# Scattering expert results to token rows, and max tiles of 512 and 205 keys under a new head order

## What is computed

```python
xn = layernorm(x)
# attention, 16 heads of 16: all 2048 queries, but only 717 keys are allowed
cam = (pos < 205) | (pos >= 2048 - 512)
attn = softmax(where(cam, (rope(q) @ rope(k).T) / 4, -inf))
a = (attn @ v) @ Wo.T + bo
# experts: 8 of them, inner width 176, each token goes to its best one
expert, weight = top-1 index of (xn @ router.T), first of softmax(top 2)
f = weight * ((silu(gate[expert](xn)) * up[expert](xn)) @ down[expert].T)
out = x + a + f
```

## Time and profile before

| | busy us | share of the span |
|---|---|---|
| TensorE matmul (PE) | 370.9 | 94% |
| VectorE (DVE) | 322.2 | 82% |
| ScalarE (ACT) | 270.2 | 68% |
| GpSimd (POOL) | 65.6 | 17% |
| chain that ended last: on PE | | 83% |
| TensorE clock granted | 0.996 on average | |

### The profile page before, as it was taken

One profiled execution on the slowest core, in us unless ns is written; L12 is line 12 of the kernel. 1 busy time (PEld: TensorE's weight loads), 2 busy tenths in 40 slices (PEclk: granted clock), 3 DMA queues, 4 the chain that ended last, 5 costly groups with the idle time before them and its releaser, 6 DMA issues.

```text
span 394.7 us, 12245 instructions
## 1 busy us (share of the span) xinstructions
PE 370.9 (94%) x4646; PEld 194.1 (49%) x4646; DVE 322.2 (82%) x549; ACT 270.2 (68%) x537; POOL 65.6 (17%) x82
## 2 busy tenths in 40 slices
PE   0999999999999999999999999999999999997896
PEld 0765566766655443444444444445454444432265
DVE  5769789997759888988888888888888898874566
ACT  2534666564448878778787787878888888886910
POOL 5003734431000213032130321300000000000000
PEclk9999999999999999999999999999999999998999
DMA  7998556755111213032130321302102022095626
GB/s 238 407 384 215 145 169 200 215 171 157 41 58 54 70 32 95 11 94 63 41 88 14 99 55 46 92 11 71 55 21 70 25 52 56 17 204 105 101 54 213
DMA packets 30920, 42.53 MB, mean 108 GB/s; under 512 B 10724, under 2 KB 25700, under 8 KB 30048
## 3 DMA queue, kind: packets, MB, share of 16 engines
q1 hardware_dynamic: 29000, 36.71, 32.5%
q0 software_dynamic: 1872, 5.11, 5.1%
HBM read 27.75 MB, written 13.67 MB: 105 GB/s over the span
## 4 chain that ended last, share of the span: by engine, by line
PE 83%; DMA 5%; DVE 4%; issue 3%; ACT 2%; SPq 2%; DVEq 0%; ACTq 0%
PE ps L735 19%; PE ps L713 18%; PE ps L653 17%; PE ps L601 7%; PE ps L528 5%; PE ps L614 5%; PE ps L772 4%; DVE mx L1025 3%; DMA softmax_sums<-o_st 2%; DMA bqk<-bqk_in 2%; PE ps L639 2%; PE ps L517 1%; PE ps L587 1%; PE ps L626 1%; PE ps L510 1%
## 5 line engine op out<-in xcount | busy, mean ns | idle before, releaser
L1025 DVE TENSOR_REDUCE mx<-ps 128x1 f32<-128x717 f32 x232 | 198.6, 899 | 30.6 <-PE ps L653 30.1
L735 PE MATMUL ps<-q_op,k_op 98*32 98x512 bf16 (+1 forms) x1472 | 129.7, 383 | 3.6 <-DMA q_op<-neg_row 1.6
L1307 ACT ACTIVATE probs<-ps 128x512 f32<-128x512 f32 x192 | 103.1, 598 | 19.9 <-PE ps L735 18.1
L653 PE MATMUL ps<-k_op,q_op 96*32 96x512 bf16 (+1 forms) x1856 | 111.2, 315 | 0.4 <-DVE mx L1025 0.3
L653 PEld LDWEIGHTS ps<-k_op,q_op 96*32 96x32 bf16 x1856 | 50.7, 96 | 56.3 <-issue 25.3
L735 PEld LDWEIGHTS ps<-q_op,k_op 98*32 98x32 bf16 (+1 forms) x1472 | 42.3, 96 | 67.0 <-ACT probs L1307 15.0
L713 PE MATMUL ps<-probs,v_op 128*32 128x512 f32 x384 | 50.6, 595 | 0.2 <-ACT o_st L1298 0.2
L1307 ACT ACTIVATE dn<-ps 77x512 f32<-77x512 f32 x64 | 34.8, 595 | 11.6 <-PE ps L735 11.6
L457 POOL COPY v_op<-v_all 128x192 f32<-128x192 f32 x16 | 7.0, 446 | 202.7 <-PE ps L713 202.7
L1307 ACT ACTIVATE gu<-ps 128x512 f32<-128x512 f32 x64 | 34.5, 599 | 9.1 <-PE ps L735 9.1
L1307 ACT ACTIVATE wqk<-ps 128x512 f32<-128x512 f32 x64 | 33.5, 599 | 8.1 <-PE ps L735 8.1
(11 more groups left out here) (127 smaller groups left out, 366.0 us busy)
## 6 DMA issues: line engine op xcount, KB each, us to landing
q_parts<-parts SPq DMA_DIRECT2D x12, 256.0 KB
sorted_results<-ys SPq DMA_DIRECT2D x23, 128.0 KB
q_op<-q_parts SPq DMA_DIRECT2D x15, 192.0 KB
gu<-gu_in SPq DMA_DIRECT2D x1, 2816.0 KB, 13.7
tab<-tab_in SPq DMA_DIRECT2D x1, 2048.0 KB, 11.6
sorted_rows<-xn SPq DMA_DIRECT2D x4, 512.0 KB, 6.1
out<-x_sb SPq DMA_DIRECT2D x8, 256.0 KB, 2.4
q_op<-q_parts SPq DMA_DIRECT2D x15, 128.0 KB
```

The lines of the kernel that those rows point to most:

```text
L653: ins = pe.matmul(ps[r:r + CW, at + c0:at + c0 + n], q_op[slot][0:KR, P * t + r:P * t + r + CW], k_op[slot][0:KR, c0:c0 + n], start=True, ...
L735: ins = pe.matmul(bank(4 + u % RING)[r:r + w, :], k_op[k][:, c0 + r:c0 + r + w], q_op[k][:, QB * b:QB * b + QB], start=True, stop=True)
L1025: dve.tensor_reduce(mx[:, slot, t:t + 1], ps[:, at:at + NK], AX.X, ALU.max).then_inc(max_reduced, 1)
L1307: act.activation(prob[c][0:rows, QB * b:QB * b + QB], bank(4 + u % RING)[0:rows, :], ACT.Exp, scale=SCALE).then_inc(exp_done, 1)
```

## The change

- Expert results. POOL scatters the rows of slot t with an indirect DMA from `ys` to the token's own row of `y_dram`; rows that hold no token go to row 0, and tokens have rows 1 to 2048. `result_row` holds these indices; `token_of` is the same less one, floored at zero. The scatters lag eight slots behind the gathers on POOL, each waits for its `ys` and for the landing of the scatter before. In the heads SP loads `y_dram` plainly to `y_tok` in four DMAs of 512 KB, two after `head_step(0)` and two after `head_step(1)`; on POOL only the bias add is left.
- Max tiles. The 512-column part of a tile is a step of its own (M, banks 0 and 1 by turns), the 205-column parts of two neighbouring tiles are one step (N, bank 2), and the turn of the negated maxima is a step (T), with bank 3 to itself. VectorE takes 16 maxima over 512 and 8 over 2 x 205 per head, and joins the two sets in one 16-element instruction (`join`).
- The head order, and one of its own for head 14, in which only eight M and four N remain. ScalarE copies the last head's output after unit 3 instead of unit 4.
- SP: the `load_attn` of heads 0-7 goes behind `head_step(14)`.

The core of the diff:

```diff
-ORDER = ("MSMSSSMP" + "MSMSSSMP" + "SMMSSP" + "SMSMSSSMP" + "MSMSSSMP" + "SMMSSSP")
+ORDER = ("SMSMSNSMP" + "MNSSMSMP" + "NSSMSMNSP" + "SMMSSNSP" + "TMSSMNSSMSMP" + "SNSMSMSNP")
+ORDER_14 = ("SMSMSNSMP" + "MNSSMSMP" + "NSSMSMNSP" + "SSTSSP" + "SSSSP" + "SSSSSP")
+LAG = 8
...
-            def store_ys(t):
-                sp.wait_ge(ys_ready, t + 1)
-                sp.dma_start(y_dram[t * P:t * P + P, :], ys[t % XR][:]).then_inc(ys_stored[t % XR], 16)
+            def load_results(g):
+                rows = y_dram[1 + 4 * P * g:1 + 4 * P * (g + 1), :].rearrange("(t p) d -> p t d", p=P)
+                sp.dma_start(y_tok[:, 4 * g:4 * g + 4, :], rows).then_inc(results_in, 16)
...
             for s in range(2, NSLOT):
-                store_ys(s - 2)
...
             load_neg(0, 0)
-            for t in range(NSLOT - 2, NSLOT):
-                store_ys(t)
             head_step(0, 0, first=True)
+            for n in range(XR):
+                sp.wait_ge(ys_stored[n], 16 * len(range(n, NSLOT, XR)))
+            for g in range(2):
+                load_results(g)
             head_step(1, 1)
+            for g in range(2, 4):
+                load_results(g)
...
+            head_step(14, 2, load=False)
             load_attn(0, HEADS // 2, attn_in[0])
-            head_step(14, 2, load=False)
             load_attn(HEADS // 2, HEADS - 2, attn_in[1])
...
+            def scatter(t):
+                pool.wait_ge(ys_ready, t + 1)
+                if t > 0:
+                    pool.wait_ge(ys_stored[(t - 1) % XR], ((t - 1) // XR + 1) * 16)
+                pool.indirect_dma_start(
+                    out=y_dram, out_offset=bass.IndirectOffsetOnAxis(ap=result_row[:, t:t + 1], axis=0),
+                    in_=ys[t % XR][:], in_offset=None
+                ).then_inc(ys_stored[t % XR], 16)
...
+            for t in range(LAG, NSLOT + LAG):
+                if t < NSLOT:
+                    gather(t)
+                scatter(t - LAG)
...
-            def gather_result(t):
-                pool.indirect_dma_start(
-                    out=y_tok[:, t, :], out_offset=None, in_=y_dram,
-                    in_offset=bass.IndirectOffsetOnAxis(ap=row_of[:, t:t + 1], axis=0)
-                ).then_inc(gathered, 16)
+            def add_bias(t):
                 pool.tensor_tensor(x_sb[:, t, :], x_sb[:, t, :], bvo[:, HID:2 * HID], ALU.add
...
-            def max_tile(h, t, slot):
-                pe.wait_ge(max_reduced, h * NT + t - 1)
-                at = 1024 * (t % 2)
-                if t == 3:
-                    pe.wait_ge(neg_copied, h)
-                if t == 1:
-                    turn_neg(h - 1, (slot - 1) % RING)
-                for c0, n in ((0, 512), (512, NK - 512)):
+            def max_wide(h, t, slot):
+                if wide_count(h, t) >= 2:
+                    pe.wait_ge(wide_reduced, wide_count(h, t) - 1)
+                for r in range(0, P, CW):
+                    ins = pe.matmul(bank(t % 2)[r:r + CW, :], q_op[slot][0:KR, P * t + r:P * t + r + CW],
+                                    k_op[slot][0:KR, 0:NWIDE], start=True, stop=True)
+                ins.then_inc(wide_scored, 1)
+            def max_tail(h, pair, slot):
+                if tail_count(h, pair) >= 1:
+                    pe.wait_ge(tail_reduced, tail_count(h, pair))
+                for n in range(2):
+                    t = 2 * pair + n
                     for r in range(0, P, CW):
...
+                                        k_op[slot][0:KR, NWIDE:NK], start=True, stop=True)
+                ins.then_inc(tail_scored, 1)
...
-            def reduce_tile(h, t, slot):
-                dve.wait_ge(max_scored, h * NT + t + 1)
-                at = 1024 * (t % 2)
-                dve.tensor_reduce(mx[:, slot, t:t + 1], ps[:, at:at + NK], AX.X, ALU.max
+            def reduce_pair(h, pair, slot):
+                for t in (2 * pair, 2 * pair + 1):
+                    dve.wait_ge(wide_scored, wide_count(h, t) + 1)
+                    dve.tensor_reduce(mx[:, slot, t:t + 1], bank(t % 2)[:, 0:NWIDE], AX.X, ALU.max
+                                      ).then_inc(wide_reduced, 1)
+                dve.wait_ge(tail_scored, tail_count(h, pair) + 1)
+                dve.tensor_reduce(mx_tail[:, slot, 2 * pair:2 * pair + 2],
+                                  bank(2)[:, 0:2 * NTAIL].rearrange("p (t n) -> p t n", t=2), AX.X, ALU.max
+                                  ).then_inc(tail_reduced, 1)
+            def join(h, slot):
...
+                dve.tensor_tensor(mx[:, slot, :], mx[:, slot, :], mx_tail[:, slot, :], ALU.max
...
             def head_step(h, k, rest_of_next=True, start_after=True, early=False):
                 if rest_of_next:
-                    for t in range(NT // 2, NT):
-                        reduce_tile(h + 1, t, (k + 1) % RING)
+                    for pair in range(NT // 4, NT // 2):
+                        reduce_pair(h + 1, pair, (k + 1) % RING)
+                    join(h + 1, (k + 1) % RING)
                     negate(h + 1, (k + 1) % RING)
...
-                    if u == NQB and not first:
+                    if u == NQB - 1 and not first:
                         copy_o(h - 1, (k - 1) % RING)
```

More of the change, by code:

```diff
@@ L461, in _ @@
             pool.wait_ge(token_ready, 1)
-            for t in range(NSLOT):
+            def scatter(t):
[6 more added lines that the diff above has]
+                ).then_inc(ys_stored[t % XR], 16)
+            for t in range(LAG):
                 gather(t)
-                if t == 6:
+                if t == LAG - 2:
                     pool.wait_ge(v_read, NCH)
@@ L718, in head_step @@
             def head_step(h, k, first=False, rest_of_next=True, start_after=True):
-                u = j = p = 0
-                for what in ORDER:
+                u = j = pair = p = 0
+                for what in ORDER if start_after or not rest_of_next else ORDER_14:
                     if what == "S":
@@ L744, in head_step @@
                                 pe.wait_ge(qk_loaded, (h + 3) * LOADS)
[L745 to L747 removed]
+                            max_wide(h + 2, j - NT // 2, (k + 2) % RING)
+                        j += 1
+                    elif what == "N":
+                        if pair < NT // 4 and rest_of_next:
+                            max_tail(h + 1, NT // 4 + pair, (k + 1) % RING)
+                        if pair >= NT // 4 and start_after:
+                            max_tail(h + 2, pair - NT // 4, (k + 2) % RING)
+                        pair += 1
+                    elif what == "T":
+                        if rest_of_next:
                             turn_neg(h + 1, (k + 1) % RING)
[L749 removed]
                     else:
@@ L827, in _ @@
             step(dve.memset(tiles_upto[:], 0.0))
+            step(dve.memset(mx_tail[:], -3.0e38))
             moments(0)
@@ L1126, in head_step @@
                 if start_after:
-                    for t in range(2, NT // 2):
-                        reduce_tile(h + 2, t, (k + 2) % RING)
+                    for pair in range(1, NT // 4):
+                        reduce_pair(h + 2, pair, (k + 2) % RING)
                 if not (isinstance(h, int) and h == 0):
```

54 lines of the change are left out of this document (29 added, 25 removed).

## The result

The changed kernel takes 407.5 us (median of 4 runs, 404.99 to 408.52) against 395.19 us (394.01 to 395.59): a ratio of 1.032, interval 1.027 to 1.037. The change makes the kernel 12 us slower. 391.4 us was predicted, with a range that ended at 397.0. A few executions fall in a slower state of the chip; the ratios in this text leave them out, the medians do not.

A forecast was written before the change was run, and what follows sets the result against it. The prediction took TensorE to bound the kernel (83% of the chain). Heads -4.8, gathers -4.15, plain loads +1.2, expert steps 0 and end +4.0 sum to -3.75 us, giving 391.4 us against the median; range 382.5 to 397.0.

The forecast's parts named there:

- The expert steps: Expert stage: 23 stores become scatters on POOL, at no cost; 0 us, bounds -1 to 7.1.
- Rival (d): Expert steps: scatters disturb them as gathers did the heads, 0.31 us each, 7.1 us; 398.5 us in all, chance 0.1.
- The plain loads: Start of head 2: two result loads push back operand loads; +1.2 us once, bounds 0 and 2.8.
- A steady head: Heads 1 to 14: new order and split maxima give 15.6 us per head for 15.97; -4.8 us over 13 intervals.
- The gathers: Heads 1 to 8: result gathers leave, the bias add keeps 0.1 us per head; -4.15 us of 4.95.
- The end: From head 14 on: joined attention loads delay the last divide, and TensorE idles, then runs at half clock; +4.0 us.
- (a): Rival: the end is clean and follows TensorE, -4.5 us instead of +4.0; 382.9 us in all, chance 0.2.
- (b): Rival: heads gain nothing from the order, VectorE or operand loads hold 15.97 us; 396.2 us in all, chance 0.15.
- (c): Rival: any POOL work costs the heads, so the bias add keeps all 4.95 us; 395.5 us in all, chance 0.1.

The follow-up runs named there:

- e3: The changed kernel, with each slot's empty rows scattered to a row of their own and no scatter waiting for the one before; 401.43 us, ratio 1.011.
- e6: e3 with the second pair of result loads issued in the middle of head step 1, behind load_neg(2); 397.08 us, ratio 1.004.
- e7: e3 with SyncE's queue re-ordered: result loads as in e6, store_recip behind operand loads, attention loads spread over heads 11 to 14; 388.36 us, ratio 0.983.
- e1: The kernel before with only the expert result path changed (scatters, plain loads, no result gathers), heads and order as before; 408.78 us, ratio 1.032.
- e5: e3 with load_attn of heads 0 to 7 put back ahead of head step 14; 395.95 us, ratio 1.004.
- e8: e2 with SyncE's queue re-ordered in the same way as in e7; 388.13 us, ratio 0.982.
- e2: The changed kernel with expert results stored and gathered as before, leaving new order, split maxima and moved load_attn; 398.06 us, ratio 1.007.
- e4: The changed kernel with six result buffers (ys) for four, scatters still waiting for each other; 408.2 us, ratio 1.034.
- e11: e7 with six result buffers for four; 384.11 us, ratio 0.984, on a chip where the kernel before took 390.03 us.
- e9: The kernel before with a second, unread gather of the same rows in each expert step; 399.13 us, ratio 1.024.
- e10: The kernel before with GpSimd filling a spare, unread tile twice in each expert step; 390.42 us, ratio 1.001.

## Why the prediction was wrong

**The expert steps, predicted 0 with 7.1 at most, measured +11.6** (+5.2 in the steps, +6.4 from the last gate-up product to head 0). This step failed, and it alone turns the sign: -3.75 + 11.6 is +7.9. The sentence that failed is that "`ys` has four buffers, and scatter t lands well before slot t+4 is written". It was held against one scatter's landing, not against the rate of a chain of them. "Each waiting for the scatter before" was written down and not priced: issue to landing 3.42 us and 0.73 to the next, 3.84 us on average, in steps of 2.5 to 3.2. e3 shows 7.3 us of it directly. The 0.94 us of the earlier trace rows is GpSimd's part of a transfer, not the transfer. The page of before gives no landing for an indirect one, but a scatter moves 128 KB, and the nearest row, the 128 KB load of `xnT` from `attn_out`, has 3.1 us from issue to landing. 3.1 us and a hand-over of some 0.3, against steps of 2.5 to 3.2 us, would have given 23 x 3.4 = 78 us of scatters (by the measured rate 88) for 67 us of steps, and the right sign. Rival (d) had the right stretch and sign, with a disturbance of 0.31 each as mechanism; the 4.4 us that e3 still loses are near its size, but come as a few pauses of over 1 us, and their cause is not shown.

**The plain loads, +1.2, measured about +4.5.** The place and the mechanism were right (operand loads pushed back), the size was out of its bounds (0 to 2.8). Head 2 to 3 takes 20.03 for 15.5. The loads begin at 164.20, 1.4 us behind the results' issues, but the last operand then takes 4.54 us to land beside 1 MB in the same queue. In the traces e6 gets 3.8 us back there. The first two loads did not come in the middle of head 0 either: SyncE waited for the last scatter and issued them at 144.17, 10.5 us behind its P.

**A steady head, 15.6, measured 15.47 or 15.48, twice 15.6 to 15.7**: -6.1 over 13 intervals instead of -4.8, from 15.5 each. What was laid out by hand (15.45) was closer than the 0.2 added for late loads; but heads 11 to 13, of 16.26, 16.01 and 15.58, take 1.4 back, with operand loads behind `store_recip`, as the text had it for every third head. e7, with the loads ahead of it, shows 15.47 to 15.60 there.

**The gathers, -4.15**: the 4.95 us went entirely (e1), so the bias add keeps nothing. Beside the GpSimd adds the reductions of VectorE lose no time, which is what the Trainium skill says in "SBUF — State Buffer", section "Who interferes with whom"; the trace agrees, with 15.96 us per head in e1 with and without them. So the late start in the earlier trace rows came with the gather.

**The end, +4.0, measured +2.3** from head 14's start (353.82) to the end, 52.7 us for 50.4 (+3.2 from its second P, which the new order puts earlier in the step). Point by point: head 15 follows without a wait, as forecast (13.94 us from P to P). The sums of head 14 are read back at 382.97, 29.1 us after head 14's start (31.2 forecast); the last divide begins at 39.8 (41.6 forecast). But the path was not the forecast one, in which `invert(14)` waits for those sums. VectorE comes to `invert(14)` without any wait, straight from the 16 adds of the expert results, and these stood behind the first divide, which waited for the reciprocals of heads 0 to 7:

```profile
377.06 2.50 DVE L1192 TENSOR_TENSOR xnT<-xnT,tab 128x512 f32<-128x512 f32 x4 [14.06 <-DMA tab<-softmax_recips]
379.47 6.42 DVE L1204 SCALAR_TENSOR_TENSOR x_sb<-xn,tk_weight,x_sb 128x256 f32<-128x256 f32 x16
385.81 0.25 DVE L1163 RECIPROCAL recip_c<-sum_c 128x16 f32<-128x16 f32 x1
```

The sums had landed at 384.68, about 1 us sooner, so that the time came out near is in part luck; in e3 it is the sums that VectorE waits for, 1.15 us. TensorE idles 3.93 us between the halves of the projection (over 5 forecast) and pays with the clock (VectorE's last divide, TensorE behind it, and the stretch's row, in which 0.57 is the granted clock, half clock for most of it):

```profile
393.66 2.54 DVE L1192 TENSOR_TENSOR xnT<-xnT,tab 32x512 f32<-32x512 f32 x4 [2.00 <-DMA tab<-o_st]
```
```profile
394.40 2.07 PE L808 MATMUL ps<-wo,xnT 128*128 128x256 f32 x4 [3.93 <-DVE xnT L1192]
```
```profile
394.00:398.00 4.00, 3.60 (x9) 2.95 (x10) 2.88 (x5) 0.00 (x0) 0.00 (x0) 0.57 0.07 16
```

What the text also missed is that the move of `load_attn` was not needed for this: by e5 a shorter head 14 is enough, and the load can stay where it was.

Of the rivals, (a) is what e7 and e8 come to, an end that follows TensorE, with SyncE's queue mended; (b) and (c) fell with e2 and e1. One slip in the working changes nothing: TensorE done with the first half is 28.5 + 7.0 = 35.5, not 35.9.

## What to carry to other kernels

Where a change makes transfers wait for one another, price the chain by its rate, issue to landing plus the hand-over, times their number, against the time of a step; buffers only defer it, and whoever waits for the last one pays (e4). Here the scatters shared one dummy row and were made to wait for one another; with a dummy row for each slot, for two more small operations, the wait could go, 7.3 us. Whether it could have gone with the shared row was not run. When compute in a loop gets shorter, read the DMA issue queue again: its order alone was worth 11 us here (e7 against e3, by their ratios).

## What the hardware showed that was not expected

An indirect scatter of 128 rows of 1 KB takes 2.4 to 4.2 us from issue to landing (after, e4, e11), for about 1.1 us that its engine is busy, so only overlapped ones keep a step of 2.5 us. On three chips engines that have nothing to do with the indirect transfers are delayed beside them: 0.3 us for each in the heads, and single pauses of 1 to 2.9 us of several engines at once where two overlap in each step. On a fourth chip neither was seen, in one trace each of e9, e10 and e11, and the same kernel before took 390.0 us for 395. GpSimd being busy does not do it (e10). What in the transfers does it, and why one chip is free of it, stays open.
